# Time crystal moved into the scan's loop in groups of 512 tokens, and query rows of diagonal attention turned once with two of three copies on VectorE

## The reference, cut to what the change touches

The input has 2 sequences (b) of 2048 tokens with 128 channels. The program is a chain of blocks. `h` is the layer norm of the input; `masks` come from a small router over the mean of `h`.

## Time and profile before

| | |
|---|---|
| median of 3 runs | 4777.99 us (4777.87 to 4790.24) |
| the profiled execution's own time | 4793.12 us |
| its span, first to last instruction | 4791.7 us |
| TensorE, VectorE, ScalarE, GpSimd busy | 79%, 71%, 63%, 17% of the span |
| mean granted TensorE clock | 0.802 of full speed |
| phase M, up to its last `dve_out` | to 492.1 us |
| phase T, to the first load of phase C | 492.2 to 595.0 us |
| phase F, the scoring of all tiles | 2659.3 to 3984.3 us |

### The profile page before, as it was taken

One profiled execution on the slowest core, in us unless ns is written; L12 is line 12 of the kernel. 1 busy time (PEld: TensorE's weight loads), 2 busy tenths in 40 slices (PEclk: granted clock), 3 DMA queues, 4 the chain that ended last, 5 costly groups with the idle time before them and its releaser, 6 DMA issues.

```text
span 4791.7 us, 79083 instructions
## 1 busy us (share of the span) xinstructions
PE 3775.5 (79%) x31382; PEld 2000.9 (42%) x31382; DVE 3397.6 (71%) x5328; ACT 3000.6 (63%) x4964; POOL 816.1 (17%) x1094
## 2 busy tenths in 40 slices
PE   6999558768779996899998566666666665899998
PEld 5666323223234443566666111111111112567666
DVE  6778476476430004778887899999999995778787
ACT  4665136536534333466665799999999994466665
POOL 2445000000047761000000111111111110000000
PEclk8999569869889998999999555555555556999999
DMA  1000000000032210000000000000000000000000
GB/s 43 1 1 1 3 0 1 1 1 1 12 78 37 35 18 20 8 13 4 8 2 6 1 1 1 1 1 1 1 1 1 1 1 20 6 15 2 11 2 19
DMA packets 49886, 45.22 MB, mean 9 GB/s; under 512 B 21203, under 2 KB 34910, under 8 KB 49502
## 3 DMA queue, kind: packets, MB, share of 16 engines
q1 hardware_dynamic: 49518, 40.16, 4.1%
HBM read 29.52 MB, written 2.23 MB: 7 GB/s over the span
## 4 chain that ended last, share of the span: by engine, by line
PE 43%; DVE 27%; issue 10%; ACT 9%; DMA 1%; SPq 0%; POOL 0%; DVEq 0%; ACTq 0%; POOLq 0%
DVE d_negmax L2402 11%; PE psum L1902 7%; PE psum L1931 6%; PE psum L1917 5%; DVE f_m_E L2047 5%; PE psum L1537 5%; PE psum L1560 4%; ACT d_junk L2464 4%; PE psum L1154 2%; PE psum L1143 2%; PE psum L1128 2%; ACT wl_p L1375 2%; DVE f_pT_E L2066 1%; DVE wl_negmax L1280 1%; PE psum L2334 1%
## 5 line engine op out<-in xcount | busy, mean ns | idle before, releaser
L2402 DVE TENSOR_REDUCE d_negmax<-psum 128x1 f32<-128x1024 f32 x1024 | 1184.7, 1216 | 101.3 <-PE psum L2334 101.3
L2464 ACT ACTIVATE d_junk<-psum,d_negmax 128x1024 bf16<-128x1024 f32 x1024 | 1137.8, 1128 | 75.8 <-DVE d_negmax L2402 68.1
L2334 PE MATMUL psum<-d_qT,d_kT 64*128 64x512 bf16 x2048 | 605.6, 600 | 440.6 <-ACT d_junk L2464 424.3
L2153 ACT ACTIVATE hidden<-psum,f_nm_E 128x1024 f32<-128x1024 f32 x512 | 566.5, 1113 | 144.0 <-DVE f_nm_E L2050 143.8
L2047 DVE TENSOR_REDUCE f_m_E<-psum 128x1 f32<-128x1024 f32 x512 | 602.4, 1218 | 47.9 <-PE psum L1902 47.6
L1902 PE MATMUL psum<-f_k_E,f_q_swapped_E 64*128 64x512 f32 x1024 | 525.7, 622 | 6.6 <-ACT hidden L2153 6.6
L1902 PE MATMUL psum<-f_k_E,f_q_E 64*128 64x512 f32 x1024 | 525.7, 622 | 2.5 <-DMA f_q_swapped_E<-f_q_E 1.2
L1931 PE MATMUL psum<-f_pT_E,f_v_E 128*64 128x128 f32 x8192 | 504.1, 276 | 2.5 <-DVE residual L2077 2.5
L2160 ACT COPY f_pT_E<-psum 128x512 f32<-128x512 f32 x512 | 300.1, 586 | 317.7 <-PE psum L1917 317.6
L2066 DVE COPY f_pT_E<-psum 128x512 f32<-128x512 f32 x512 | 351.7, 687 | 159.0 <-PE psum L1917 148.3
L2334 PEld LDWEIGHTS psum<-d_qT,d_kT 64*128 64x128 bf16 x2048 | 105.5, 101 | 858.3 <-ACT d_junk L2464 805.9
(11 more groups left out here) (318 smaller groups left out, 5194.8 us busy)
## 6 DMA issues: line engine op xcount, KB each, us to landing
moe_gates_on_all<-moe_gate_spill SPq DMA_DIRECT2D x8, 2048.0 KB, 16.1
f_q_swapped_E<-f_q_E SPq DMA_DIRECT2D x64, 128.0 KB, 2.4
moe_w<-in_moe_w SPq DMA_DIRECT2D x8, 256.0 KB, 4.4
out<-residual SPq DMA_DIRECT2D x1, 2048.0 KB, 8.7
residual<-in_hidden_states SPq DMA_DIRECT2D x2, 768.0 KB, 7.0
residual<-in_hidden_states SPq DMA_DIRECT2D x2, 256.0 KB, 3.6
m_taps<-in_m_conv SPq DMA_DIRECT2D x4, 128.0 KB
level_sums<-in_c_sums SPq DMA_DIRECT2D x1, 512.0 KB
```

What stands on the lines that cost most here:

```text
L2153: A.activation(pb[:, u % 2, f * 2 * BANK:(f + 1) * 2 * BANK], two(2 * f), ACT.Exp, bias=nm[:, u % 4:u % 4 + 1], scale=SC, accum_out=rs[:, ...
L2334: last = T.matmul(bank(2 + 2 * (at % 3) + jj), kT[half, s, jb * P:(jb + 1) * P], qT[half, s, c * BANK:(c + 1) * BANK], start=True, stop=True)
L2402: V.tensor_reduce(mh[:, t % 2, n // 2, n % 2:n % 2 + 1], two(2 + 2 * (at % 3)), X, ALU.max, negate=True).then_inc(*maxed.up(at))
L2464: A.activation(junk[:, at % 3, :], two(2 + 2 * (at % 3)), ACT.Exp, bias=mh[:, t % 2, n // 2, n % 2:n % 2 + 1], accum_out=sh[:, t % 2, n // ...
```

```diff
-def build(nc, a, out, shape, phases=("M", "T", "C", "D", "E", "F", "E2")):
+def build(nc, a, out, shape, phases=("M", "C", "D", "E", "F", "E2")):
...
                 for i in ks:
                     if i + 1 < SK:
                         ring += [("sum", i + 1, j) for j in range(4)]
+                    if i >= 10 and i % SLOTS in (2, 3):
+                        ring += [("tln" if i % SLOTS == 2 else "tc", i // SLOTS - 1, b) for b in bs]
...
+                ring += [(kind, NG - 1, b) for kind in ("tln", "tc") for b in bs]
...
+                    SP.dma_start(tw[:, :], a["tc_w"]).then_inc(*ld.one())
+                    SP.dma_start(tbias[:, :], a["tc_b"].rearrange("(o n) -> o n", o=1)).then_inc(*ld.one())
+                    SP.dma_start(th[:, :], wide(a["tc_theta"].rearrange("(o n) -> o n", o=1), 0, P)).then_inc(*ld.one())
+                    with nc.allow_non_contiguous_dma("one gain and one bias per channel"):
+                        for n, t in enumerate(("ln_g", "ln_b")):
+                            SP.dma_start(t_gain[:, n:n + 1], a[t][1, :].rearrange("(p o) -> p o", o=1)).then_inc(*ld.one())
+                    for n, t in enumerate(("ln_g", "ln_b")):
+                        SP.dma_start(t_rows[:, n, :], bcast(a[t][1, :], P)).then_inc(*ld.one())
...
+                def pe_t_ln(g):
+                    T.wait_ge(*t_normed(g))
+                    for b in bs:
+                        bk = pe_ring("tln", g, b)
+                        for q in range(4):
+                            last = T.transpose(bank(bk)[:, q * P:(q + 1) * P], tn[:, 4 * b + q, :], ident[:, :])
+                        last.then_inc(*t_turned.up(g, b))
+
+                def pe_t_out(g):
+                    T.wait_ge(*t_chan(g, NB - 1))
+                    for b in bs:
+                        bk = pe_ring("tc", g, b)
+                        for q in range(4):
+                            o = bank(bk)[:, q * D:(q + 1) * D]
+                            T.matmul(o, chans[:, b, PAD + (4 * g + q) * P:PAD + (4 * g + q + 1) * P], tw[:, :], start=True, stop=False)
+                            last = T.matmul(o, ones[0:1, :], tbias[:, :], start=False, stop=True)
+                        last.then_inc(*t_made.up(g, b))
...
+                        if i >= 10 and i % SLOTS == 2:
+                            pe_t_ln(i // SLOTS - 1)
+                        if i >= 10 and i % SLOTS == 3:
+                            pe_t_out(i // SLOTS - 1)
...
+                    pe_t_ln(NG - 1)
+                    pe_t_out(NG - 1)
...
+                def dve_t_close(g):
+                    V.wait_ge(*faded_in(g))
+                    V.wait_ge(*tanhed(g, NB - 1))
+                    vstep(V.scalar_tensor_tensor(tn[:, :, :], tanh[:, :, :], cs[:, 1:2], tn[:, :, :], ALU.mult, ALU.add))
+                    for b in bs:
+                        h = hid[:, b * NT + 4 * g:b * NT + 4 * g + 4, :]
+                        last = V.scalar_tensor_tensor(h, tn[:, 4 * b:4 * b + 4, :], mask[:, b, 1:2], h, ALU.mult, ALU.add)
+                    last.then_inc(*closed.up(g))
...
+                            dve_t_stats(i // 2 - 1)
+                        if i == 2:
+                            dve_angle()
+                        if i >= 9 and i % SLOTS == 1:
+                            dve_t_shift(i // SLOTS - 1)
+                        if i >= 12 and i % SLOTS == 4:
+                            dve_t_close(i // SLOTS - 1)
...
+                def act_t_normed(g):
+                    A.wait_ge(*t_shifted(g))
+                    if g:
+                        A.wait_ge(*closed(g - 1))
+                    for n in range(8):
+                        b, q = n // 4, n % 4
+                        last = A.activation(tn[:, n, :], hid[:, b * NT + 4 * g + q, :], ACT.Identity, bias=t_shift[:, 8 * g + n:8 * g + n + 1],
+                                            scale=t_rs[:, 8 * g + n:8 * g + n + 1])
+                    last.then_inc(*t_normed.up(g))
...
+                        if i >= 10 and i % SLOTS == 2:
+                            act_t_ln(i // SLOTS - 1)
+                        if i >= 10 and i % SLOTS == 3:
+                            act_tanh(i // SLOTS - 1)
...
+                        if i >= 8 and i % SLOTS == 0:
+                            act_t_std(i // SLOTS - 1)
+                        if i >= 9 and i % SLOTS == 1:
+                            act_t_normed(i // SLOTS - 1)
...
+                def pool_t(g):
...
+                    G.wait_ge(*t_turned(g, NB - 1))
+                    gstep(G.tensor_tensor(tn[:, :, :], tn[:, :, :], wide(t_rows[:, 0:1, :], 1, 2 * Q4), ALU.mult))
+                    G.tensor_tensor(tn[:, :, :], tn[:, :, :], wide(t_rows[:, 1:2, :], 1, 2 * Q4), ALU.add).then_inc(*faded_in.up(g))
...
-                qT = sb(st, "d_qT", [2 * ROWS, 2, NH * P], BF16)
+                qT = sb(st, "d_qT", [2 * ROWS, 2, NH * P // 2], BF16)
...
-                    for k in range(4):
-                        u = uk if k >= 2 else uq
-                        if k == 2:
+                    for k in range(3):
+                        u = uk if k else uq
+                        if k == 1:
                             T.wait_ge(*k_spread(t))
                         rows = bank(pe_side("rows", t, k)).bitcast(BF16)
                         for q in range(8):
                             for r in range(2):
+                                eighth = 8 * (k - 1 if k else r) + q
                                 last = T.transpose(rows[ROWS * r:ROWS * r + ROWS, q * P:(q + 1) * P],
-                                                   u[:, s, 8 * (k % 2) + q].rearrange("p n x -> p (n x)"), identb[:, :])
+                                                   u[:, s, eighth].rearrange("p n x -> p (n x)"), identb[:, :])
...
-                    V.wait_ge(*turned(t, 0))
-                    if t >= 2:
-                        V.wait_ge(*scored((t - 1) * STEPS - 1))
-                    rows = bank(side_bank("rows", t, 0)).bitcast(BF16)
-                    V.tensor_copy(qT[:, s, 0:8 * P], rows).then_inc(*row_dve.up(t))
-                    yield
+                    for k, dst in enumerate((qT[:, s, :], kT[:, s, 0:8 * P])):
+                        V.wait_ge(*turned(t, k))
+                        if t >= 2:
+                            V.wait_ge(*scored((t - 1) * STEPS - 1))
+                        V.tensor_copy(dst, bank(side_bank("rows", t, k)).bitcast(BF16)).then_inc(*row_dve.up(t, k))
+                        for _ in range(3):
+                            yield
...
-                        A.copy(dst[:, s, (k % 2) * 8 * P:(k % 2 + 1) * 8 * P], rows).then_inc(*row_act.up(t, k))
+                    for _ in range(20):
+                        yield
+                    A.wait_ge(*turned(t, 2))
+                    if t >= 2:
+                        A.wait_ge(*scored((t - 1) * STEPS - 1))
+                    A.copy(kT[:, s, 8 * P:16 * P], bank(side_bank("rows", t, 2)).bitcast(BF16)).then_inc(*row_act.up(t))
                     yield
```

211 lines of the change are left out of this document (98 added, 113 removed).

## The result

The changed kernel takes 4716.25 us (median of 4 runs, 4715.77 to 4718.90); the kernel before, run beside it, 4784.11 (4777.87 to 4793.48). The ratio is 0.9858, with a 95% interval of 0.9837 to 0.9879: faster by 1.4%. The prediction had said 4713 us, faster. The profiled execution has a time of 4715.77 and a span of 4714.4 us, 77.3 less than the 4791.7 of before.

What follows compares the result with a forecast made beforehand. It took phase T as a serial chain, the scan as bound by TensorE, and VectorE and ScalarE as nearly equally busy in diagonal attention. T's side -42 and diagonal attention -23 gave 4778 - 65 = 4713 us, 80% range 4675 to 4750.

Steps and rivals of the forecast that it cites:

- T removed: Phase T, a serial chain between scan and phase C, goes with its barriers and loads: -102.7 us.
- start: Kernel start: seven loads issued ahead delay the entries behind them in SyncE's queue; +2.5 us, bounds 0 and 6.
- tail: Last group behind the scan's loop, without cover and with the clock down: 23 us, at full clock 17.
- One group in the loop: Scan: a time crystal group, three times; ScalarE wait, transposes, bank wait, products and clock drop sum to 11.0 us each.
- the products: Scan, TensorE: a group's 32 records of products, 5.1 us, taken nearer the output projection's price than T's half-clock stretch.
- first load of C near 534 us: Sign to look for: phase C's first load near 534 us instead of 595.
- What was said to be hidden: Scan: Sqrt's load and root, tanh, GpSimd's passes, VectorE's closing add nothing; statistics, theta and Sin's table stick out by 2 us.
- rival 3: The scan hides less of GpSimd's passes, statistics and VectorE's closing: 22 us dearer, 4735 us; chance 0.10.
- Diagonal attention: A tile falls from 41.5 to 40.8 us by fewer ScalarE copies: -23 us, bounds +20 and -44.
- 1 (VectorE becomes the bound, +20): Diagonal attention gets slower, TensorE's waits not being the copies' fault: +20 instead of -23, 4756 us; chance 0.13.
- 2 (waits vanish wholly): Diagonal attention's waits around the copies vanish wholly: 4692 us; chance 0.14.
- 4 (the clock stays down for the rest of the scan): Scan: new waits lower TensorE's clock from step 10 on, 22 steps, 163 us, so 4876 us; chance 0.05.

Runs made afterwards that it cites:

- bias_128_rows: Changed kernel with the time crystal's bias added by a product over 128 rows of 1/128 instead of one row; 4691.39 us.
- rows_later: Changed kernel with the bias over 128 rows and the group's normalising, transposes, products and closing one step later; 4679.10 us, ratio 0.9782 to the kernel before.
- rows_later_three: Changed kernel with bias over 128 rows, group one step later and all three diagonal-attention copies on VectorE; 4679.46 us, ratio 0.9781.
- group_later: Changed kernel with a group's normalising, transposes, products and closing one step later; 4710.29 us, ratio 0.9851.
- f_only: Kernel before with only diagonal attention changed; 4754.19 us, ratio 0.9937.
- t_only: Changed kernel with the old diagonal attention, so only the scan's new phase M is in; 4751.03 us, ratio 0.9926.
- f_act_two: Changed kernel, but of diagonal attention's three copies ScalarE makes two and VectorE one; 4727.26 us, single run.
- f_dve_three: Changed kernel with all three copies of turned rows in diagonal attention on VectorE, none on ScalarE; 4713.37 us, single run.
- after: The changed kernel itself, both parts in, against the kernel before; 4716.25 us, ratio 0.9858.
- f_four_two_two: Changed kernel, but query rows turned twice as before (four parts), two copies each on VectorE and ScalarE; 4733.86 us, single run.
- bias_first: Changed kernel with the same products reordered: in a bank the four one-row products first, then the four with 128 rows; 4696.18 us.

## Why the prediction was right, and where it was wrong

The time (4713 forecast, 4716.25 measured) is inside the range, and the direction of both parts is right. But two terms were off by about 10 us in opposite directions, and the close hit owes something to that.

*T removed, start, tail.* -102.7 stands. The start was +0.8 instead of +2.5, inside its bounds: ScalarE waited 8.21 us for the same last load instead of 6.87, but had come to it earlier. The tail was +22.9 against 23, by its own terms, here in the timeline behind the last `dve_mix`:

```profile
540.12 3.18 ACT L883 ACTIVATE tc_normed<-hidden,tc_shift,tc_rstd 128x128 f32<-128x128 f32 x8 [0.47 <-DVE tc_shift L755]
543.36 1.97 PE L482 MATMUL psum<-ident,tc_normed 128*128 128x128 f32 x8 [5.61 <-ACT tc_normed L883]
546.20 0.80 PE L491 MATMUL psum<-tc_w,normed_channels 128*128 128x128 f32 x2 [0.87 <-ACT normed_channels L890]
...
557.05 0.79 PE L492 MATMUL psum<-tc_b,ones 1*128 1x128 f32 x2
557.88 0.60 ACT L896 ACTIVATE tc_tanh<-psum 128x512 f32<-128x512 f32 x1 [5.19 <-PE psum L492]
```

Normalising 3.18 us, transposes and copies 2.84 until the first product at 546.20, products 11.6 at half clock until 557.8, tanh 0.6, then VectorE's 1.28 and 1.42. "At full clock 17" had the right size for another reason: with 128 rows the tail came to 27.4 - 9.6 = 17.8 us (`bias_128_rows`), 17.2 (`rows_later`) and 16.9 (`rows_later_three`), where the alternation is gone and the clock, 0.56 to 0.66 over the products, is still mostly down.

*One group in the loop.* Forecast 11.0 us, measured 16.5, 16.9 and 12.0 (steps 9 to 16, 17 to 24, 25 to 30), 15.1 on average. (Of the 16.5, 1.1 lies in step 16, which in other executions of the same code was up to 1.6 us shorter than before; the third group has no convolution behind it.) **This is the step that failed**, and in it one term: the products. I took 5.1 us, by the output projection's 0.14 us a record, and held the clock's drop to 1.2 us and to the wait for ScalarE. Measured in step 11: 8.8 us for the products, and 1.73, 0.47 and 0.29 us more for the three matmul groups behind them (3.68, 1.07 and 3.10 instead of 1.95, 0.60 and 2.81): 11.3 us where the forecast had 5.1 + 1.2 = 6.3. (Of the step's +12.3 the last 1.0 isn't in one row.) Neither row on which the price rested showed the two kinds of matmul in turns at full clock; T's own stretch did, at half clock, and I read its 0.36 us a record as the clock's doing alone. At half clock `rows_later` takes 0.43 us for what takes 0.72 in the kernel after, so more than a third of that price was the alternation. Where it is absent, in `bias_128_rows`, steps 10 and 11 grow by 5.5 and 5.0 us, which is the "about 5 and 5" of the forecast, and a group costs 10.5 us against 11.0. There the clock did fall behind the wait (225.53 to 232.36 us), as the forecast had it.

The wait for ScalarE's eight instructions was 3.74 us (3.2 + 0.67 forecast), the transposes 1.04, the wait for a bank ahead of the convolution 0.43 (0.5 taken). `group_later` takes the first away: step 10 grew by 0.8 instead of 3.1 to 5.5, and the loop by 9.7 us less.

The mark "first load of C near 534 us" didn't follow from my own sum, which gives 595.0 - 42 = 553; it came at 561.45.

*What was said to be hidden* was, but for one table load. GpSimd's passes took 2.4 us, not 3.38, VectorE's closing 1.25 + 2 times 0.75, statistics 0.29 and 0.17 us each. The rows of GpSimd's second pass and of the statistics stand below; step 12, with the closing in it, has the length of before to 0.01 us.

```profile
L1038 POOL TENSOR_TENSOR tc_normed<-tc_normed,tc_rows 128x1024 f32<-128x1024 f32 x3 | 7.4, 2472 | 0.2
L743 DVE BATCH_NORM_STATS2 m_ln_stats<-hidden 128x6 f32<-128x128 f32 x30 | 7.3, 285 | 0.5
```

Steps 0 to 9, which carry statistics at each even one, theta and the two sines, grew by 0.03 us together (-1.6 to +1.8 in the other runs, `f_only` without these instructions among them). So the 2 us put down for them were not needed, and rival 3 with its 22 us didn't come: the loop's excess is TensorE's, not VectorE's or GpSimd's.

*The table loads.* In the loop ScalarE's loads of 1.28 us were followed by the next activation at 0.01 to 0.02 us (208.22 behind 206.92 + 1.28), as the earlier trace rows had said. The prediction counted seven more loads in the loop; there are four (60 against 56), and none of them stands ahead of a tanh. In the first two groups they cost nothing that shows. In the third, where no silu and no convolution cover it, Sqrt's load and the load of exp's table behind it make TensorE's fronts wait 0.66 us at 454.77 (no wait before the change), and step 25 is 1.1 us longer in every run with the new phase M: the "if the cover goes, 1.5 us" of the forecast.

*Diagonal attention.* -34.4 us against -23, beyond the forecast and inside its bounds (-44). The mechanism was right: turning once and moving a copy each take waits of TensorE, and so of VectorE, away. The groups of VectorE's maxima and ScalarE's exponentials in the kernel after:

```profile
L2475 DVE TENSOR_REDUCE d_negmax<-psum 128x1 f32<-128x1024 f32 x1024 | 1180.1, 1210 | 52.5 <-PE psum L2406 52.5
L2534 ACT ACTIVATE d_junk<-psum,d_negmax 128x1024 bf16<-128x1024 f32 x1024 | 1135.9, 1118 | 91.8 <-DVE d_negmax L2475 84.1
```

And VectorE's timeline over parts of one tile:

```profile
3002.28 0.68 DVE L2468 COPY d_qT<-psum 128x1024 bf16<-128x1024 bf16 x1
3002.88 3.47 DVE L2475 TENSOR_REDUCE d_negmax<-psum 128x1 f32<-128x1024 f32 x3
...
3012.04 10.27 DVE L2475 TENSOR_REDUCE d_negmax<-psum 128x1 f32<-128x1024 f32 x9 [0.56 <-PE psum L2406]
3023.07 1.23 DVE L2475 TENSOR_REDUCE d_negmax<-psum 128x1 f32<-128x1024 f32 x1 [0.76 <-PE psum L2406]
...
3037.95 1.22 DVE L2475 TENSOR_REDUCE d_negmax<-psum 128x1 f32<-128x1024 f32 x1 [0.30 <-PE psum L2406]
```

A tile has waits of 0.56, 0.76 and 0.30 us, 1.62 in all, against the 1.67 forecast, and the two that belong to the projection and the closing product stayed as they were the earlier trace rows (here 3023.07 and 3037.95). Off was the price of VectorE's work. I added durations: 0.68 for the copy, and counted the base as 41.5. But an instruction that follows without a wait starts before the one ahead has ended: the copy starts at 3002.28, the next maximum at 3002.88, so it costs 0.60, and where a wait has gone two more instructions overlap by 0.08. From first to last maximum, 31.97 tiles, VectorE was busy 1224.8 us before and 1237.0 after, +0.38 a tile, and idle 97.2 and 50.6, -1.46 a tile: together -1.08, which is the -34.4. The waits were forecast at 3.1 down to 1.67, nearly as measured. The mis-sized term is the copy with its overlaps: +0.70 taken, +0.38 measured.

*The rivals.* 1 (VectorE becomes the bound, +20) fell: VectorE is busy 96% of the phase, but it had waits to lose. 2 (waits vanish wholly) didn't come, though the time saved was nearer its 44 than my 23. 3 fell for its cause. 4 (the clock stays down for the rest of the scan) had the right resource and mostly the wrong trigger, and the wrong length: the clock fell within the products of three groups (8.8, 8.9 and 7.7 us for each list) and once behind the wait (step 18, 3.4 us), and was back at 1.00 from 389.9 to 478 us. By my own mark ("wrong if a group costs more than 15 us") two of three groups say that the reasoning was wrong there, 5.5 and 5.9 us above the 11.0. The other two marks stayed clear: 1.64 us of VectorE's waits a tile, and a clock of 0.95 in the scan.

## What to carry to other kernels

Before one-row products (a bias, a row of ones) are put into a busy TensorE list, sort them: all one-row products of a bank first, or one over the whole bank, or the same term over 128 rows. Here that saved 16 to 25 us of 4716, most with 128 rows, where the clock never fell within the products of the loop. When work is moved into a loop, place it by the engine that is late in that step: the same eight ScalarE instructions cost 3.7 us of TensorE's time in step 8g+10 and none a step later, where steps 8g+10 and 8g+11 are each 0.8 us longer than before. And price an instruction in a queue by the distance between starts, not by its duration.

## What was not expected of the hardware

- TensorE's granted clock fell from 1.00 to its lower level in the middle of an unbroken list (begun at 246.17, fallen by 249.93), while matmuls took turns between 128 rows and one, in all three groups of the loop (0.78, 0.78, 0.82) and in `group_later` too. With the one-row products sorted or joined it fell in the third group only, and with 128 rows or no bias in none.
- Those turns cost time at full clock as well: 0.42 us a pair of records against 0.22 with 128 rows throughout and 0.27 sorted (4.34 us for 16 pairs), since no weight load that changed the number of rows ran beside the matmul ahead of it.
- After its wait of 3.74 us in step 10 the decays' matmul took 1.99 us for 8 records, as without a wait; after the same 3.74 us in step 18 it took 3.46, and in the kernel before a convolution behind a wait of 3.13 us was slow. A wait alone doesn't tell what the clock will do, and executions of the same code differ: in step 10 it fell in `t_only`, `f_act_two` and `f_dve_three` and not in `after` and `f_four_two_two`.
- VectorE's product of two tiles beside GpSimd's new pass took 2.46 us, the same instruction in the kernel before, with GpSimd idle, 0.43 (at 256.32 us; 0.42 to 0.43 in all its 32 steps). It cost nothing, since VectorE then waited for TensorE.

```profile
248.66 2.35 POOL L1037 TENSOR_TENSOR tc_normed<-tc_normed,tc_rows 128x1024 f32<-128x1024 f32 x1
248.83 2.46 DVE L712 TENSOR_TENSOR m_state_faded<-m_state,m_decay 128x256 f32<-128x256 f32 x1
```

The Trainium skill ("GPSIMD Engine Reference", Specifications) says that GpSimd shares its way to memory with VectorE instructions that read two tiles; this pair of rows agrees.

`bias_first` is 6 us longer than `bias_128_rows` in the loop although its products' step is only 0.5 longer. Steps 0 and 8 have 3.3 us of that, and the same two steps differ by 1.6 and 2.8 us between executions of the same code; step 27 has 2.2, by the fall of the clock shown above. Left open: why the clock falls there, and whether the last group can be cut in halves, so that its first half runs in the loop at full clock. That wasn't tried.
